# Third attention: scores in four row tiles, eight heads to a unit

## What is computed

```python
def _mha(x, in_w, in_b, out_w, out_b, mask=None):
    qkv = x @ in_w.T + in_b
    q, k, v = jnp.split(qkv, 3, axis=-1)          # then b, heads, s, 16
    scores = jnp.einsum('bhsd,bhtd->bhst', q, k) / np.sqrt(D).astype(x.dtype)
    if mask is not None:
        scores = jnp.where(mask[None, None], -jnp.inf, scores)
    attn = jax.nn.softmax(scores, axis=-1)
    out = jnp.einsum('bhst,bhtd->bhsd', attn, v)
    return out.transpose(0, 2, 1, 3).reshape(b, s, e) @ out_w.T + out_b
...
local_mask = jnp.abs(idx[:, None] - idx[None, :]) > WINDOW     # WINDOW = 5
x = x + _mha(x, l_..., mask=local_mask) + _mha(x, g_...)
x = _layernorm(x, ln1_g, ln1_b)
```

## Time and profile before

| | before |
|---|---|
| median of 3 runs | 451.59 us (451.37 to 452.58) |
| span of the profiled execution | 449.9 us |
| TensorE / VectorE / ScalarE / POOL busy | 95% / 50% / 33% / 5% |
| third attention: first scores to last attend | 101.52 to 162.97 us |
| granted TensorE clock, mean of the span | 0.998 |

### The profile page before, as it was taken

The page is one execution under the profiler, slowest core; times in us unless marked ns, Lnnn a source line. Parts: engine busy times, 40 slices in busy tenths (PEclk is TensorE's granted clock), DMA queues, the critical chain, the costliest instruction groups (busy, mean ns, idle before and its releaser), DMA issues.

```text
span 449.9 us, 10013 instructions
## 1 busy us (share of the span) xinstructions
PE 429.2 (95%) x3386; PEld 347.6 (77%) x3387; DVE 223.3 (50%) x647; ACT 148.1 (33%) x304; POOL 23.9 (5%) x67
## 2 busy tenths in 40 slices
PE   5889899989999999989999999999999999999996
PEld 2546757755556577434699999999999999999995
DVE  1774564278666465799344334333433443344333
ACT  2400653445454423232223223222323222323231
POOL 7300000006000000200000000000000000000000
PEclk9999999999999999999999999999999999999999
DMA  7300002600000000000650567716771145517250
GB/s 258 121 2 0 1 1 75 205 1 0 1 1 1 0 3 1 0 0 2 194 181 0 186 190 255 260 40 195 268 257 25 26 161 180 193 43 266 64 188 24
DMA packets 32584, 43.57 MB, mean 97 GB/s; under 512 B 1202, under 2 KB 26420, under 8 KB 32436
## 3 DMA queue, kind: packets, MB, share of 16 engines
q1 hardware_dynamic: 32564, 43.31, 29.6%
HBM read 43.05 MB, written 0.26 MB: 96 GB/s over the span
## 4 chain that ended last, share of the span: by engine, by line
PE 87%; DVE 8%; DMA 2%; ACT 1%; issue 1%; SPq 0%; DVEq 0%; ACTq 0%
PE bank L990 27%; PE bank L1004 14%; PE bank L945 4%; PE bank L745 3%; PE bank L683 3%; PE bank L673 3%; PE bank L486 2%; PE bank L774 2%; PE bank L789 2%; PE bank L919 2%; PE bank L760 2%; PE bank L569 2%; PE bank L909 2%; PE bank L911 2%; DMA rows<-in_rows 2%; PE bank L960 1%
## 5 line engine op out<-in xcount | busy, mean ns | idle before, releaser
L990 PEld LDWEIGHTS bank<-shared_room,w 128*128 128x128 f32 x1100 | 128.7, 192 | 2.9 <-issue 0.5
L990 PE MATMUL bank<-shared_room,w 128*128 128x128 f32 x1100 | 130.9, 275 | 0.0
L1726 DVE TENSOR_TENSOR shared_room<-bank,shared_room 128x512 f32<-128x512 f32 (+1 forms) x75 | 48.4, 645 | 39.3 <-PE bank L990 39.3
L1201 ACT ACTIVATE shared_room<-bank 128x512 f32<-128x512 f32 (+1 forms) x75 | 42.1, 562 | 78.0 <-PE bank L990 78.0
L1004 PE MATMUL bank<-w,shared_room 128*128 128x128 f32 (+1 forms) x550 | 66.8, 277 | 0.0
L1004 PEld LDWEIGHTS bank<-w,shared_room 128*128 128x128 f32 (+1 forms) x550 | 63.4, 192 | 0.0
L1734 DVE SCALAR_TENSOR_TENSOR ye_lo<-bank,slot_weight,ye_hi 128x128 fp32r<-128x128 f32 x25 | 8.8, 351 | 71.4 <-ACT ye_hi L1207 71.4
L1707 DVE TENSOR_SCALAR pick_bf<-slot_no,place 128x128 bf16 x104 | 22.8, 282 | 23.5 <-issue 23.5
L486 PE MATMUL bank<-ones_bf 128*128 128x512 bf16 x144 | 34.2, 379 | 0.0
L1147 ACT ACTIVATE p<-bank,nmax 128x256 f32<-128x256 f32 (+1 forms) x64 | 22.6, 420 | 29.3 <-DVE nmax L1555 29.2
L1027 ACT ACTIVATE spread<-bank 128x512 fp32r<-128x512 f32 x26 | 15.5, 597 | 31.5 <-PE bank L955 31.5
(11 more groups left out here) (350 smaller groups left out, 512.1 us busy)
## 6 DMA issues: line engine op xcount, KB each, us to landing
w<-in_w SPq DMA_DIRECT2D x34, 682.5 KB, 4.8
w<-in_w SPq DMA_DIRECT2D x17, 640.0 KB
shared_room<-in_experts SPq DMA_DIRECT2D x8, 257.0 KB, 6.2
w<-in_sw SPq DMA_DIRECT2D x2, 682.5 KB, 5.8
l<-in_l SPq DMA_DIRECT2D x1, 1164.0 KB, 10.2
rows<-in_rows SPq DMA_DIRECT2D x1, 780.0 KB, 6.8
w<-in_w SPq DMA_DIRECT2D x17, 42.5 KB
w<-in_sw SPq DMA_DIRECT2D x1, 640.0 KB
```

Source lines behind the costliest of these rows:

```text
L990: last = mm(bank[b][:, SLOTS * (t - t0):SLOTS * (t - t0 + 1)], w[p][:, 128 * t:128 * t + 128], xe[:, p, :], start=True, stop=True)
L1201: nc.scalar.activation(silu[:, slot, 0:n], bank[slot][:, 0:n], ACT.Silu)\
L1726: tt(he[:, p, t0:t1, :].rearrange("p t s -> p (t s)"), bank[2 + slot][:, 0:n], silu[:, slot, 0:n], ALU.mult).then_inc(sem("he_ready"), 1)
```

## The change

- Eight heads are a unit, 10 units in all, 5 for each image: two global query tiles, the edge, two local windows.
- The rows are four tiles of 32, which hold an even and an odd head each. The queries are kept twice, once with the odd heads' rows at zero and once with the even heads' (`q3[s][half]`, made by ScalarE with a mask of the pair as scale and a masked bias). The keys are taken as they are; `km3` and its 32 copies of keys by head are gone.
- scores(u) is 8 products, 4 row tiles for each half, tile r into bank r: 256 columns each for a global unit, 128 for a local one. The band is added first, by four products of 256 columns. They all wait until the exponentials of unit u - 1 have left banks 0 to 3.
- largest(u) is four instructions, one for each bank; exps(u) eight.
- A global unit is turned in four groups through banks 6 and 7, a local one in two. `p3T` has four slots. The last group of a unit is copied by ScalarE, behind the unit's exponentials, the others by VectorE.
- TensorE's order for a unit: the groups that may go ahead (three of a global unit, one of another), the scores of the next unit, the first attend of a global unit, the other groups, the other attends. Denominators, spread quotients and projections stand at units 3, 5, 6 and 8.
- Query and key products of both sides come first; values go to banks 5, 6 and 7.

In the lists below, `vg`, `ob` and `nmax` are the values, the attended result and the maxima; line numbers are those of each kernel.

The core of the diff:

```diff
-        km3 = [[room("keys", [128, HEADS, PIX]) for b in range(B)] for s in "gl"]
+        q3 = [[room("keys", [128, N]) for half in range(2)] for s in "gl"]
...
             def scores(u):
-                if u >= 2:
-                    pe.wait_ge(sem("exp3"), u - 1)
+                if u:
+                    pe.wait_ge(sem("exp3"), PART_AT[u])
...
-                    mm(bank[u % 2][:, :], q3[0][:, b * PIX + 128 * t:b * PIX + 128 * t + 128],
-                       km3[0][b][:, h:h + GLOBAL_HEADS, :], start=True, stop=True).then_inc(sem("score3_mm"), 1)
+                if kind == "l":
+                    for r in range(ROWS4):
+                        mm(bank[r][:, 0:2 * n], ident_bf[:], band[:].unsqueeze(1).broadcast_to([128, 2, n]),
+                           start=True, stop=False, skip_group_check=True)
+                for half in range(2):
+                    for r in range(ROWS4):
+                        rows4 = slice(32 * r, 32 * r + 32)
+                        last = mm(bank[r][:, n * half:n * half + n], q3[s][half][rows4, queries:queries + 128],
+                                  k3[s][rows4, keys:keys + n], start=(kind == "g"), stop=True,
+                                  tile_position=(32 * r, 0), skip_group_check=True)
+                last.then_inc(sem("score3_mm"), 1)
...
+            for u, (kind, b, _) in enumerate(UNITS):
+                ahead = 3 if kind == "g" else 1
+                for g in range(min(ahead, TURNS[kind])):
+                    turn(u, g)
+                if u + 1 < len(UNITS):
+                    scores(u + 1)
+                if u in (3, 5, 8):
+                    denominators((3, 5, 8).index(u))
+                if u == 6:
+                    project(0, 0)
+                    project(0, 1)
+                attend_first = kind == "g"
+                if attend_first:
+                    attend(u, 0)
+                for g in range(ahead, TURNS[kind]):
+                    turn(u, g)
+                for a in range(1 if attend_first else 0, ATTENDS[kind]):
+                    attend(u, a)
+                if u in (3, 5, 8):
+                    spread_quotients((3, 5, 8).index(u))
...
+            def copy_turned(u, g):
+                n = TURN_AT[u] + g
+                act.wait_ge(sem("p3T_mm"), n + 1)
+                if n >= TURN_SLOTS:
+                    act.wait_ge(sem("attend3"), attend_of(*TURN_LIST[n - TURN_SLOTS]))
+                copy(p3T[:, n % TURN_SLOTS, :], bank[6 + n % 2][:, :]).then_inc(sem("p3T_act"), 1)
...
+            for u, (kind, _, _) in enumerate(UNITS):
+                if u in (2, UNITS_B, UNITS_B + 2):
+                    copy_out((2, UNITS_B, UNITS_B + 2).index(u))
                 exps(u)
+                for g in BY_ACT[kind]:
+                    copy_turned(u, g)
             copy_out(3)
```

More of the change, by code:

```diff
@@ L765, in turn @@
[L765 to L770, removed]
+                    return
+                s = "gl".index(kind)
+                n = PIX if kind == "g" else 128
+                queries = b * PIX + (128 * t if kind == "g" else WINDOWS[t][0])
@@ L793, in attend @@
+            def attend(u, a):
+                kind, b, t = UNITS[u]
+                for g in ((2 * a, 2 * a + 1) if kind == "g" else (a,)):
+                    wait_copied(TURN_AT[u] + g)
+                if b and kind == "g" and t == 0 and a == 0:
+                    pe.wait_ge(sem("ob3_ready"), 1)
+                if b and kind == "e":
+                    pe.wait_ge(sem("u3_added"), 1)
+                if kind == "e":
                     _, first, end = WINDOWS[t]
-                    turned = p3T[0:EDGE_K, u % 2, 0:EDGE].rearrange("p (q h) -> p q h", h=HEADS)
+                    turned = p3T[0:EDGE_K, TURN_AT[u] % TURN_SLOTS, 0:EDGE].rearrange("p (q h) -> p q h", h=HEADS)
@@ L1509, in _ @@
             keys(0)
-            dve.wait_ge(sem("k3_ready"), 1)
-            def global_keys(heads):
-                for h in heads:
-                    ts(km3[0][0][:, h, :], k3[0][:, 0:PIX], head_mask[:, h:h + 1], None, ALU.mult)\
-                        .then_inc(sem("km3_global0"), 1)
-            global_keys(range(2 * GLOBAL_HEADS))
+            keys(1)
             def values(dst, src, side, n):
@@ L1601, in add_attention @@
                 dve.wait_ge(sem("att3_mm"), b + 1)
-                settle(tt(flat(own), bank[4 if b else 7][:, 0:PIX], flat(own), ALU.add))
-            add_attention(0)
+                settle(tt(flat(own), bank[1 if b else 5][:, 0:PIX], flat(own), ALU.add))
+            for u, (kind, _, _) in enumerate(UNITS):
+                largest(u)
+                if u == 0:
+                    global_values()
+                    local_values()
+                    edge_queries()
+                if u in (4, 6, 9):
+                    divide((4, 6, 9).index(u))
+                for g in range(TURNS[kind]):
+                    if g not in BY_ACT[kind]:
+                        copy_turned(u, g)
+                if u in (3, 5, 8):
+                    invert((3, 5, 8).index(u))
+                if u == 6:
+                    add_attention(0)
+                    dve.sem_inc(sem("u3_added"), 1)
             measure(LN_MID3, tiles_of(u3), range(NT // B), gain=row("ln1_g"))
@@ L1812, in spread_heads, with pair_columns @@
         return out.reshape(2, 128, v.shape[1]).transpose(1, 0, 2).reshape(128, 2 * v.shape[1])
+    def pair_columns(v):
+        out = np.zeros((2, HEADS // 2, 2, HD), np.float32)
+        for half in range(2):
+            out[half, :, half, :] = v.reshape(HEADS // 2, 2, HD)[:, half, :]
+        return out.reshape(2, C).T
     parts = {"ffn1": a["L3_attn_ffn_w1"].T,
```

297 lines of the change are left out of this document (134 added, 163 removed).

## The result

| | before | changed |
|---|---|---|
| median, same chip | 452.05 us (451.37 to 452.58, 4 runs) | 457.31 us (452.84 to 459.12, 4 runs) |
| ratio | | 1.010 [1.006, 1.014] |
| span of the profiled execution | 449.9 us | 450.7 us (this run took 452.84) |
| granted TensorE clock, mean of each run's span | 0.998 in the profile | 0.986, 0.971, 0.968, 0.964 |

The kernel became slower. I forecast 449.3 us, faster. The four runs differ among themselves by 1.4%, where those of before lie within 0.3%, and they lie in the order of their clock: spans of 450.7, 453.8, 456.6 and 456.9 us at clocks of 0.986, 0.971, 0.968 and 0.964. The profile shows the mildest of the four. The others are known by their time and mean clock alone.

The account below looks back on a forecast made before the run. TensorE bounds the kernel before; afterwards a three-engine chain binds the third attention. Its laps put the last attend at 160.29 instead of 162.55 us, so 451.59 - 2.26 = 449.3 us; own range 447.8 to 450.8, wider range 446.3 to 454.

Parts of the forecast that it names:

- The sum: Third attention: first exponential at 104.09 us plus 56.20 us of laps gives the last attend at 160.29, against 162.55 before.
- rival 3: Third attention: TensorE's idle time lowers its clock, costing 2.3 us a lap for two laps, 453.9 us; chance 0.07.
- The sign that I had named: Listed as showing the forecast wrong: a granted TensorE clock below 1.00 in the third attention.
- the price of a lap: Clock rival's cost in the third attention: passes take nearly twice as long, 2.3 us a lap.
- The chain: Third attention: exponentials, scores, attend, turn and ScalarE's copy bind across three engines; a global lap 6.08 us against 8.3.
- The score step: Four row tiles run abreast: global step 1.19 us held, 1.25 to its result; local 1.21 held, 1.28 to its result.
- Rival 2: Score step: weight loads of row tiles stand in line, 8.2 us dearer in all, 457.5 us; chance 0.12.
- Rival 1: Some 20 mode changes on the path cost 0.19 us each instead of 0.09: no change, 451.1 us; chance 0.15.
- Rival 4: The chain is looser than added: score steps at 0.6 us give 3 us more, 446.3 us; chance 0.11.
- streaming term: Global score step: 2 halves x 2 passes of 256 columns at 0.22 us, 0.88 us; 1.13 by the skill's 3.07.
- Work that lay aside: Removed key copies lay beside TensorE, except VectorE's first two, counted in unit 0; they and the added small work: 0.

Follow-up runs that it names:

- e1_warm: Changed kernel plus sixteen bf16 products of no use in TensorE's waits (values wait, units 3, 5, 8): 449.62 us, ratio 0.9945 to the kernel before.
- e6_warm_half: As e1_warm, with two products of no use in place of four at each of the four places: 453.09 us, ratio 1.0003 to the kernel before.
- e7_warm_late: As e1_warm, but the twelve products of units 3, 5 and 8 stand ahead of the last turned group, not the first: 459.25 us, ratio 1.0155.
- e2_full_rows: Changed kernel with each row-tiled score product replaced by one over all 128 rows and a quarter of the columns: 461.55 us, ratio 1.0206.
- e3_turn_first: Changed kernel with the last group turned directly behind the next scores and denominators inverted behind the next unit's maxima: 450.03 us, ratio 0.9957.

## Why the prediction was wrong

**The step that failed is the clock.** The sum took every TensorE term at the full clock, and gave rival 3, "The clock falls", a chance of 0.07. The sign that I had named, a granted clock below 1.00 in the stage, is what the profile shows. What I put against it was one window, 192.0 to 195.5 us, busy 2.05 of 3.50 at a clock of 1.00. One pause that ends is not a stage in which pauses recur in each lap: in 118.2 to 134.7 us the changed kernel was busy 11.09 of 16.50, a larger share than that window's, and the clock fell. My own estimate of 13 us of idle time in the stage was near (61.50 - 47.01 = 14.5 in the profile) and should have weighed more than one window. That the falls follow from the holes is shown by the sets of runs: e1_warm (holes filled, mean clocks 0.989 and up), e6_warm_half (half filled, about half the effect), e7_warm_late (same products elsewhere, clocks as without them) and e2_full_rows (no row-tiled scores, clock down). Where a fall begins is not fixed: it began at 134.7 us here, at 109.1 in e3_turn_first, with TensorE's work the same up to there. Which of TensorE's work counts as activity, turns and narrow products among it, no run separates.

The Trainium skill, "TensorE: Matmul & The Clock Gate", section "A second HAM failure mode: psum-queue depth-cycling", says that short idle spells between groups of products, often enough, make the clock swing between its levels. The trace agrees, with holes of 0.3 to 1.7 us before the falls, and by that rule rival 3 would have stood far above 0.07.

**Of its size, the price of a lap was too high and the time at half clock too short.** I gave 2.3 us for each of two laps, 453.9 us. The differences of first exponentials in the profiled run:

| to unit | 1 | 2 | 3 | 4 | 5 | 6 | 7 | 8 | 9 | last attend |
|---|---|---|---|---|---|---|---|---|---|---|
| forecast | 8.20 | 6.61 | 2.27 | 5.72 | 5.77 | 6.98 | 9.15 | 2.27 | 5.71 | 3.52 |
| measured | 8.27 | 6.56 | 2.24 | 5.67 | 5.62 | 8.37 | 9.22 | 2.24 | 7.07 | 4.19 |

Units 6, 9 and the last attend have the half clock: +1.39, +1.36, +0.67, together 3.42 us for 10.2 us of it. The profile of e6_warm_half, at a clock of 1.00 throughout the stage, has the same laps without a fall (ScalarE and, in the last line, TensorE in order of time):

```profile
105.03 3.02 ACT L1185 ACTIVATE shared_room<-bank,nmax 128x256 f32<-128x256 f32 x8 [0.39 <-DVE nmax L1596]
...
133.39 3.02 ACT L1185 ACTIVATE shared_room<-bank,nmax 128x256 f32<-128x256 f32 x8
...
140.28 3.02 ACT L1185 ACTIVATE shared_room<-bank,nmax 128x256 f32<-128x256 f32 x8
...
151.76 2.17 ACT L1185 ACTIVATE shared_room<-bank,nmax 128x128 f32<-128x128 f32 x8 [2.06 <-DVE nmax L1596]
...
157.42 2.17 ACT L1185 ACTIVATE shared_room<-bank,nmax 128x128 f32<-128x128 f32 x8
...
161.06 0.42 PE L841 MATMUL bank<-shared_room,vl 128*32 128x123 f32 x8 [0.33 <-ACT shared_room L1067]
```

The lap to unit 6 is 6.89 us, that to unit 9 5.66, so the two falls cost 1.5 and 1.4 us there, where I had 2.3 each.

The other runs lost more. The two middle ones of the four runs have spans of 453.8 and 456.6 us at 0.971 and 0.968. The four spans rise by 6.2 us for 0.022 of mean clock, some 280 us for a whole unit, and the profiled execution is near that slope: 10.2 us at half are 5.1 / 450.7 = 0.011 of mean clock, 3.2 us. From the 0.998 of before to 0.970 it gives 7.8 us, and 447.6 + 7.8 = 455.4 is the middle of the four. A mean clock 0.028 lower is 25 us at half clock, an estimate, since those runs have no trace: two to three times the 10.2 of the profile. How much of it lay in this stage stays open, because falls between 11.7 and 20.6 us stand in five of the other profiles.

**The chain was right.** All laps at full clock are within 0.15 us of the forecast, and unit 0 came at 103.94 (forecast 104.09). Without the 3.42 us the last attend would be at 159.97; I said 160.29. In e6_warm_half, with no fall in the stage, the first exponential stands at 105.03 and the last eight passes of the attends at 161.06, 56.03 us later; the sum had 56.20. In the three runs of e1_warm with a clock of 0.994 or more the span is 446.6 to 447.5 us; 449.9 - 2.26 = 447.6 was the forecast.

**The score step.** The four passes of a group start within 0.02 us of each other. The four groups of the step at 102.00 start at 102.00, 102.32, 102.54 and 102.75: 0.32 us for the first, 0.22 for each other, as I had it (0.10 + 0.22, then 0.22). The product ahead of it would have let the next in at 101.91 (its second pass starts at 101.48 and holds 0.43), so the change of mode cost my 0.09. The next product starts at 103.08: the step holds TensorE 1.17 us, and I had 1.19; it lasts 1.15 to its result, and I had 1.25. A local one holds TensorE from 119.16 to 120.35, 1.19 (I had 1.21).

Rival 2 (loads in line) is refuted by the loads, 16 within 0.74 us. The measured 457.31 us lies at its 457.5 by chance. Rival 1 (dearer mode changes) wanted 0.19 for each change; into row tiles it was 0.09, and from row tiles to the attend's column tiles, from 110.12 to 110.45, 0.33 against the 0.22 of a group, 0.11. Rival 4 (steps of 0.6) is refuted by the same step.

In line, 16 passes of 0.217 would be 3.47 us. The streaming goes at four times that pace (0.22 a group), and the whole step, with its change of mode and its exit, at 3.47 / 1.17 = 3.0 times. The Trainium skill's 3.07 for four row tiles ("TensorE: Matmul & The Clock Gate", Part 3) is near the ratio of the whole step here, and not near that of its streaming term, to which I had applied it.

**Work that lay aside.** The copies of keys (POOL from 6.77 to 0.00 us in the stage) gave nothing by going, beyond unit 0's start, as I took it: the sum without them fits. What lies around a span was 1.7 us before and 2.1 us in the changed kernels (452.84 - 450.7); these 0.3 to 0.4 us stay unexplained.

## What to carry to other kernels

When an edit takes work from the engine that binds and gives the end to a chain of three engines, ask what the holes do to TensorE's clock before counting the gain: holes of about 1.5 us in each lap cost more here than the 2 us that the edit gave. Fill such holes with products of no use where TensorE waits anyway, and only there: the same products ahead of ready work left the clock where it was without them. Then shorten the chain. The two add up in the main: filling gave 7.7 us in the changed kernel and 5.6 in the shortened one, shortening 8.9 us without filling and 6.8 with it. Judge such a kernel by several runs, since one profile shows one pattern of falls.

## What was not expected of the hardware

- The clock fell although TensorE was never idle for longer than 1.71 us in the stage.
- How long the clock is down differs from one execution of a program to the next: the changed kernel's four runs have means from 0.964 to 0.986, and half filling gives 0.975 to 0.999.
- In e2_full_rows it stayed down from 121 to 138 us while TensorE's records are busy 15.46 of 17.00 us. This is open.
- 16 full-row float32 passes of 64 columns took 1.90 us, longer than 16 row-tiled passes of 256 columns (1.15 us). The starts of the full-row passes lie 0.11 apart, the pace of full loads, and the 16 loads of the row-tiled step all lie within 0.74 us.
- A fall nearly doubles what TensorE does alone (1.15 to 2.09 us for a score step), yet the lap to unit 6 grew only by 1.4: the clock was back at 138.1, ahead of the lap's attend and last turn. The fall cost what TensorE had on the chain while it lasted.
